# Residual loads, residual copies and output stores issued from GpSimd's DMA queue instead of the sync engine's, in a two-layer attention and FFN kernel

## The chip, the core and the metric

One Trainium2 chip, one of its cores. The metric is the device time of one execution in microseconds (us); less is better. The kernel before takes 1800.41 us (median of three runs, 1794.83 to 1801.01).

## What is computed

Sixteen independent sequences ("batches" b = 0 to 15) of 512 tokens and 128 features go through four residual steps:

```python
x = L0_attn_x                                   # (16, 512, 128) f32
x = x + _L0_attn_ref(_layernorm(x), ...)        # 16 heads of 8, softmax attention
x = x + _L0_ffn_ref(_layernorm(x), ...)         # silu(gate) * up, 384 hidden, then down
x = x + _L1_attn_ref(_layernorm(x), ...)        # 16 heads of 8, q and k RMS-normalised
x = x + _L1_ffn_ref(_layernorm(x), ...)         # base matmul + 8 gated LoRA experts of rank 8
```

Each `x +` is a residual: the value that went into the step has to be at hand when its result comes out.

## The kernel before, in words

The program is written engine by engine, by hand. Time is cut into slots of 64 units (`UNITS`); in each slot one attention `(layer, batch)` runs, in the order of `ATTENDS`: layer 0 of batches 0 and 1, then in turn layer 0 of batch b and layer 1 of batch b-2, and last layer 1 of batches 14 and 15. So in the middle two slots serve one batch. In each unit TensorE computes one 128x512 tile of scores (line 1237), ScalarE takes its exponential (L742), and TensorE multiplies it with the values (L1252); 26 units ahead of that, TensorE computes the same scores for the row maximum (L1227) and VectorE reduces them (L973). Between these units stand the "pieces" of the other steps: projections, layer norms, FFN, routing.

Every engine walks over the same unit counter t and, for each unit, issues what a table says is due: `PE_AT`, `ACT_AT`, `DVE_AT`, `POOL_AT`, `SP_AT`, one number (the unit in its group) for each piece. `due_table` turns a group's slot and the number into t. The numbers only set the order of instructions on each engine. What makes an engine wait is semaphores (`wait_ge`; `hold` on the queue that issues DMAs, which is the same wait).

Names that the change and the prediction speak of:

- `load_res0(b)`: loads x of batch b from HBM into `res[0]`, the residual of the first attention, as 128 partitions x 4 pieces of 512 bytes (256 KB). It waits until the addition that reads the same buffer for batch b-1 is done (`read["pr0"]`). Its reader is VectorE's `project_add(0)` (L1010, `x<-ps,res`).
- `copy_x2(b)`: copies x2 (the value after the first FFN) within SBUF into `res[1][b % 2]`, the residual of the second attention: 128 x 2 KB. It waits for `read["dn"]` (the addition that writes x2 of batch b) and for `read["pr1"]` of batch b-2. Its readers are `project_add(1)` of batch b and, as a guard against overwriting x2, `down_add(b + 1)`.
- `store(b)`: stores x3 of batch b to HBM, 128 x 4 pieces of 512 bytes. It waits for `read["out"]`, the final addition. `project_add(1)` of batch b+1, which overwrites x3, waits for `stored`, so for the landing of this store.
- On GpSimd (POOL): `norm_factors(k, b)` (L595 `rstd`, L597 `shift`), the factors of the four layer norms (nf0 to nf3), for which ScalarE's `apply_norm` (L748) waits; `up_mul` (L647, three for each batch); `normalise` (L616, `o_raw`), the division of an attention's result by the softmax sum; `residual1`, `residual2` (L602 to L610), `newton_round`, `scale_qk`, `mix` (L654).
- On SyncE (SP) in the kernel before: all other loads and stores of the loop, too. `max_rows` (L458) and `stack_half` (L452) feed the score matmuls, `rden_lines` (L472, L478) feeds `normalise`.

In the kernel before all three of the DMAs above stand in SP's walk:

```python
b = at(SP_DUE, "cpx2", t)
if b is not None:
    copy_x2(b)
```

and no DMA is issued by GpSimd anywhere.

Of the kernel before, what the change touches and what calls it, by code (L numbers as in the profile page):

```python
# [12 lines left out]
BATCH, SEQ, D = 16, 512, 128  # L13
# [62 lines left out]
SP_AT = {"A": {"rows0": -5, "rows1": 9, "rows2": 32, "rows3": 43, "den0": 40, "rden0": 52, "den1": 71,  # L76
# [3 lines left out]
         "S0": {"lx": 16},  # L80
         "M1": {"lr0": 52},
         "M2": {"out_p1": 21},
         "H1": {"cpx2": -16, "half0_p1": 38, "half1_p1": 42},
         "H1_tail": {"cpx2": 45, "half0_p1": 35, "half1_p1": 66},
         "E": {"store": 91}}

# [112 lines left out]
def build(nc, T, out_dram):  # L199
    ctx = ExitStack()  # L200
    with ctx:
# [167 lines left out]
        stored = sem("stored")  # L369
# [14 lines left out]
        def _(sp):  # L384
            def hold(sem, value):
                need(sp, sem, value)
# [32 lines left out]

            def load_res0(b):  # L420
                hold(read["pr0"], b)
                sp.dma_start(res_of(0, b)[:, :, :], tokens(b)).then_inc(res_copied[0], 16)

            load_res0(0)
            load_x(1)

# [54 lines left out]

            def copy_x2(b):

                hold(read["dn"], b + 1)
                hold(read["pr1"], b - 1)
                sp.dma_start(res_of(1, b)[:, :, :], x2[:, :, :]).then_inc(res_copied[1], 16)

            def store(b):

                hold(read["out"], b + 1)  # L490
                sp.dma_start(out_dram[b:b + 1].rearrange("a (t p) d -> p (a t) d", p=128), x3[:, :, :]
                             ).then_inc(stored, 16)

            parts_out(0, (0, 1), 0)
# [3 lines left out]
            for t in TIMES:  # L498
# [13 lines left out]
                if a is not None:  # L512
                    rden_lines(a[0], 1, a[1])
                b = at(SP_DUE, "lr0", t)
                if b is not None and b + 1 < BATCH:
                    load_res0(b + 1)
                b = at(SP_DUE, "out_p1", t)
# [20 lines left out]
                if a is not None:  # L538
                    max_rows(a[0], 3, a[1])
                b = at(SP_DUE, "cpx2", t)  # L540
                if b is not None:
                    copy_x2(b)
                b = at(SP_DUE, "half0_p0", t)
# [6 lines left out]
                if a is not None:  # L550
                    max_rows(a[0], 0, a[1])
                b = at(SP_DUE, "store", t)
                if b is not None:
                    store(b)
            hold(stored, 16 * BATCH)
# [3 lines left out]
        def _(pool):  # L559
# [47 lines left out]
            def residual2(l, n, b):  # L607
# [3 lines left out]
                                   ).then_inc(part2[2 * l + n], 1)  # L611

            def normalise(l, c, b):

                pool.wait_ge(rden_in[l], 16 * (2 * b + c + 1))
                pool.tensor_tensor(o_of(l, b)[:, c, :], o_of(l, b)[:, c, :], rden_all[:, c, :], ALU.mult  # L616
                                   ).then_inc(att_ready[l], 1)
# [46 lines left out]
            for n in (0, 1):  # L664
                residual1(0, n, 0)
                residual2(0, n, 0)
            norm_factors(0, 1)
            ones_in_k(1)
            clear_values(v_aug[1][0], 2)
            clear_values(v_aug[1][1], 3)  # L670
            for t in TIMES:
# [4 lines left out]
                for n in (0, 1):  # L676
                    b = at(POOL_DUE, f"sc{n}", t)
                    if b is not None:
                        scale_qk(n, b)
                a = at(POOL_DUE, "no1", t)  # L680
                if a is not None:
# [722 lines left out]
```

## Time and profile before

| | us |
|---|---|
| median of three runs (lowest, highest) | 1800.41 (1794.83, 1801.01) |
| the profiled execution: its own time | 1797.05 |
| its span, first to last instruction | 1795.3 |
| PE busy | 1684.5 (94% of the span) |
| DVE busy | 1543.6 (86%) |
| ACT busy | 1415.8 (79%) |
| POOL busy | 586.6 (33%) |
| DMA queue of SP and ACT (q1) | 27.6% of 16 engines |

How to read it: the span is what the trace shows; the execution's own time holds 1.75 us more around it. PE is TensorE, DVE VectorE, ACT ScalarE, POOL GpSimd, SP SyncE, which only issues DMAs; "SPq" is its queue. A busy share is an average over the start, the middle and the end of the kernel, which differ. The granted TensorE clock was 0.982 of full speed in the mean of this execution.

### The profile page before, as it was taken

What the parts mean: (1) busy time and instruction counts of PE and PEld (TensorE: products, weight loads), DVE (VectorE), ACT (ScalarE), POOL (GpSimd) and SP (SyncE); (2) the same over time, 40 slices, a digit from 0 to 9 for tenths busy, and PEclk for the clock granted to TensorE, in tenths of its full rate; (3) what the DMA queues carried; (4) which work ended last, traced back from release to release, by engine and by line L of the source; (5) the groups of instructions that cost most, each with busy time, mean ns of one, the idle gap of its engine ahead of it and who ended that gap; (6) DMA issues with size and microseconds to landing.
All of it is one profiled execution on the core that took longest, in us unless ns stands there. A gap on an engine that the chain in (4) does not pass through costs nothing.

```text
span 1795.3 us, 32451 instructions
## 1 busy us (share of the span) xinstructions
PE 1684.5 (94%) x10962; PEld 633.9 (35%) x10962; DVE 1543.6 (86%) x3347; ACT 1415.8 (79%) x2922; POOL 586.6 (33%) x840
## 2 busy tenths in 40 slices
PE   5999999999999999999999999999999999999995
PEld 2233333434333343333334333343433334334333
DVE  4988899898898989889898989989899898887981
ACT  2778788787978878787887988878797887777872
POOL 4224234151423324233242423415142332423311
PEclk8899999999999999999999999999999999999996
DMA  5232414223142322404232140422314142122310
GB/s 121 67 85 71 116 38 120 68 83 104 32 121 55 121 61 73 114 27 129 58 114 66 56 128 24 120 71 79 104 32 120 55 121 55 46 59 78 87 36 25
DMA packets 164024, 140.97 MB, mean 79 GB/s; under 512 B 40778, under 2 KB 145428, under 8 KB 163860
## 3 DMA queue, kind: packets, MB, share of 16 engines
q1 hardware_dynamic: 162084, 137.92, 27.6%
q8 instruction: 88, 1.44, 0.3%
q10 hardware_dynamic: 1776, 0.98, 0.2%
q14 instruction: 76, 0.62, 0.1%
HBM read 76.99 MB, written 55.57 MB: 74 GB/s over the span
## 4 chain that ended last, share of the span: by engine, by line
PE 62%; DVE 29%; issue 3%; ACT 2%; DMA 2%; SPq 1%; POOL 1%; DVEq 0%; ACTq 0%; POOLq 0%
DVE neg_max L973 20%; PE ps L1252 19%; PE ps L1237 14%; PE ps L1227 8%; PE ps L1273 7%; PE ps L1184 5%; PE ps L1266 3%; PE ps L1317 3%; DVE bn L949 2%; PE ps L1278 2%; DVE x L1010 2%; PE ps L1323 2%; DVE neg_high L979 1%; ACT probs L742 1%; DVE mv L957 1%
## 5 line engine op out<-in xcount | busy, mean ns | idle before, releaser
L973 DVE TENSOR_REDUCE neg_max<-ps 128x1 f32<-128x512 f32 x2048 | 1299.8, 682 | 100.2 <-PE ps L1227 91.1
L742 ACT ACTIVATE probs<-ps 128x512 f32<-128x512 f32 x2048 | 1093.3, 600 | 232.7 <-PE ps L1237 230.4
L1227 PE MATMUL ps<-k_stack,q_stack 48*128 48x512 bf16 x2048 | 679.1, 388 | 42.9 <-DVE neg_max L973 31.9
L1237 PE MATMUL ps<-q_stack,k_stack 50*128 50x512 bf16 x2048 | 632.1, 383 | 7.6 <-ACT probs L742 3.1
L1252 PE MATMUL ps<-probs,v_aug 128*32 128x512 f32 x4096 | 548.5, 608 | 0.7 <-ACT o_raw L718 0.7
L1237 PEld LDWEIGHTS ps<-q_stack,k_stack 50*128 50x128 bf16 x2048 | 148.1, 94 | 530.0 <-ACT probs L742 249.4
L1227 PEld LDWEIGHTS ps<-k_stack,q_stack 48*128 48x128 bf16 x2048 | 153.4, 93 | 227.4 <-DVE neg_max L973 202.1
L595 POOL TENSOR_TENSOR rstd<-vpe,half_neg 128x4 f32<-128x4 f32 x64 | 64.5, 1009 | 351.6 <-DVE vpe L964 351.5
L647 POOL TENSOR_TENSOR ht<-up,gs 128x512 f32<-128x512 f32 x48 | 61.1, 1273 | 223.2 <-ACT up L718 223.2
L1252 PEld LDWEIGHTS ps<-probs,v_aug 128*32 128x32 f32 x4096 | 80.7, 108 | 143.2 <-issue 73.7
L748 ACT ACTIVATE xn<-x,shift,rstd 128x128 f32<-128x128 f32 x192 | 80.7, 486 | 37.8 <-POOL shift L597 37.8
L616 POOL TENSOR_TENSOR o_raw<-o_raw,rden_all 128x512 f32<-128x512 f32 x64 | 81.3, 1270 | 49.9 <-DMA rden_all<-rden_rows 49.4
L602 POOL TENSOR_TENSOR qp<-qf,qp 128x512 bf16<-128x512 f32 x32 | 37.0, 1157 | 165.0 <-ACT qp L718 165.0
L654 POOL TENSOR_TENSOR coef<-gating,rm 128x64 f32<-128x64 bf16 x64 | 16.7, 292 | 225.3 <-DVE gating L1073 225.3
L1278 PE MATMUL ps<-wo,o_raw 128*128 128x128 f32 x512 | 67.3, 286 | 8.7 <-POOL o_raw L616 7.9
L626 POOL TENSOR_TENSOR nw_t<-nw_y 128x128 f32<-128x128 f32 x48 | 19.1, 399 | 156.2 <-DVE nw_y L1045 153.8
L1278 PEld LDWEIGHTS ps<-wo,o_raw 128*128 128x128 f32 x512 | 61.2, 196 | 18.3 <-issue 12.0
L1022 DVE SCALAR_TENSOR_TENSOR gs<-th,ps 128x512 f32<-128x512 f32 x48 | 32.7, 682 | 35.3 <-POOL ht L647 35.3
L1184 PE MATMUL ps<-ident,xn 128*128 128x128 f32 x256 | 44.1, 298 | 17.1 <-ACT xn L748 16.7
L718 ACT ACTIVATE up<-ps 128x512 f32<-128x512 f32 x48 | 28.7, 597 | 37.0 <-PE ps L1273 36.9
L1273 PE MATMUL ps<-xnt,w_up 128*128 128x256 f32 x192 | 54.3, 405 | 0.5 <-DVE gs L1022 0.5
L1010 DVE TENSOR_TENSOR x<-ps,x 128x512 f32<-128x512 f32 x32 | 22.0, 688 | 37.3 <-PE ps L1317 21.6
(117 smaller groups left out, 1579.5 us busy)
## 6 DMA issues: line engine op xcount, KB each, us to landing
rden_all<-rden_rows SPq DMA_DIRECT2D x64, 256.0 KB
q_rows<-qp SPq DMA_DIRECT2D x32, 384.0 KB, 2.9
k_rows<-kp SPq DMA_DIRECT2D x32, 384.0 KB, 2.9
q_stack<-q_rows SPq DMA_DIRECT2D x64, 192.0 KB, 3.8
k_stack<-k_rows SPq DMA_DIRECT2D x64, 192.0 KB, 4.8
q_stack<-q_rows SPq DMA_DIRECT2D x64, 144.0 KB, 2.9
k_stack<-k_rows SPq DMA_DIRECT2D x64, 144.0 KB, 3.3
q_rows<-qp SPq DMA_DIRECT2D x32, 256.0 KB, 3.1
```

Source lines behind the costliest of these rows:

```text
L595: pool.tensor_tensor(rstd[k][:, :], vpe[k][:, :], half_neg[:, :], ALU.pow).then_inc(rstd_ready[k], 1)
L616: pool.tensor_tensor(o_of(l, b)[:, c, :], o_of(l, b)[:, c, :], rden_all[:, c, :], ALU.mult).then_inc(att_ready[l], 1)
L647: pool.tensor_tensor(ht[:, c, :], up[:, :], gs[:, :], ALU.mult).then_inc(ht_done, 1)
L742: act.activation(probs[:, g % RING, :], home("score", (l, b, u)), ACT.Exp).then_inc(exps, 1)
L748: last = act.activation(xn[k][:, t, :], x[:, t, :], ACT.Identity, bias=shift[k][:, t:t + 1], scale=rstd[k][:, t:t + 1])
L973: dve.tensor_reduce(neg_max[l][:, pair // 2, col:col + 1], home("max", (l, b, n)), AX.X, ALU.max, negate=True).then_inc(max_taken, 1)
L1184: return pe.transpose(dst, src, ident[0:n, 0:n])
L1227: pe.matmul(home("max", (l, b, m)), q_stack[l][row:row + KROWS, pair, tok:tok + 128], k_stack[l][row:row + KROWS, pair, :], start=True, st ...
L1237: pe.matmul(home("score", (l, b, u)), k_stack[l][row:row + AROWS, pair, tok:tok + 128], q_stack[l][row:row + AROWS, pair, :], start=True, ...
L1252: last = pe.matmul(acc[32 * j:32 * j + 32, :], v_of(l, b)[:, kt, 8 * e + 2 * group + pp, :], probs[:, (g + j) % RING, :], start=(s == 0 an ...
L1273: return pe.matmul(dst[:, 256 * half:256 * half + 256], w, xt[:, 256 * half:256 * half + 256], start=True, stop=True)
L1278: last = pe.matmul(by_tile(dst)[:, t, :], o_of(l, b)[:, c, 128 * t:128 * t + 128], wo[l][:, c, :], start=c == 0, stop=c == 1)
```

## The change

The three functions move, with their waits, from SyncE's program to GpSimd's. In the tables `lr0`, `cpx2` and `store` keep their numbers and go from `SP_AT` to `POOL_AT`. The first `load_res0(0)`, which SyncE issued right after the weights, now stands on GpSimd behind the residual steps of batch 0 and ahead of the layer norm factors of batch 1. Within a unit, GpSimd issues them behind `scale_qk` and ahead of `normalise(.., 1, ..)`.

```diff
            "M1": {"nr0": 66, "nr1": 66, "nr2": 67, "nf1": 27, "um0": 27, "um1": 33, "um2": 38, "nf2": 55,
+                "lr0": 52},
...
-           "E": {"nf3": 32, "mix": 48}}
+           "E": {"nf3": 32, "mix": 48, "store": 91},
+           "H1": {"cpx2": -16},
+           "H1_tail": {"cpx2": 45}}
...
-         "M1": {"lr0": 52},
-         "H1": {"cpx2": -16, "half0_p1": 38, "half1_p1": 42},
-         "H1_tail": {"cpx2": 45, "half0_p1": 35, "half1_p1": 66},
-         "E": {"store": 91}}
+         "H1": {"half0_p1": 38, "half1_p1": 42},
+         "H1_tail": {"half0_p1": 35, "half1_p1": 66}}
...
+            def hold(sem, value):
+                need(pool, sem, value)
...
+            def load_res0(b):
+                hold(read["pr0"], b)
+                pool.dma_start(res_of(0, b)[:, :, :], tokens(b)).then_inc(res_copied[0], 16)
+
+            def copy_x2(b):
+
+                hold(read["dn"], b + 1)
+                hold(read["pr1"], b - 1)
+                pool.dma_start(res_of(1, b)[:, :, :], x2[:, :, :]).then_inc(res_copied[1], 16)
+
+            def store(b):
+
+                hold(read["out"], b + 1)
+                pool.dma_start(out_dram[b:b + 1].rearrange("a (t p) d -> p (a t) d", p=128), x3[:, :, :]
+                             ).then_inc(stored, 16)
...
                 residual2(0, n, 0)
+            load_res0(0)
             norm_factors(0, 1)
...
+                b = at(POOL_DUE, "cpx2", t)
+                if b is not None:
+                    copy_x2(b)
+                b = at(POOL_DUE, "store", t)
+                if b is not None:
+                    store(b)
+                b = at(POOL_DUE, "lr0", t)
+                if b is not None and b + 1 < BATCH:
+                    load_res0(b + 1)
```

The same functions and calls are taken out of SyncE's program. Three places on GpSimd, in the order in which its instructions stand (semaphores that each waits for in brackets; line numbers of the changed file differ, so L647 is L645 there, L595 is L570, L616 is L614).

**GpSimd, first FFN of batch 0, before.** `ht` is `up_mul`; the first `rstd` pair is nf0 of batch 3, the second nf2 of batch 0.

```order
L647 TENSOR_TENSOR ht<-up,gs 128x512 [waits u2_read,g2_read]
L595 TENSOR_TENSOR rstd<-vpe,half_neg 128x4 [waits var_ready0]
L597 TENSOR_TENSOR shift<-neg_mean,rstd 128x4 [waits rstd_ready0]
L595 TENSOR_TENSOR rstd<-vpe,half_neg 128x4 [waits var_ready2]
L597 TENSOR_TENSOR shift<-neg_mean,rstd 128x4 [waits rstd_ready2]
```

**The same place in the change:**

```order
L645 TENSOR_TENSOR ht<-up,gs 128x512 [waits u2_read,g2_read]
L603 DMA res<-x 128x512 [waits dn_read]
L570 TENSOR_TENSOR rstd<-vpe,half_neg 128x4 [waits var_ready0]
L572 TENSOR_TENSOR shift<-neg_mean,rstd 128x4 [waits rstd_ready0]
L597 DMA res<-in_L_attn_x 128x4x128 [waits pr0_read]
L570 TENSOR_TENSOR rstd<-vpe,half_neg 128x4 [waits var_ready2]
L572 TENSOR_TENSOR shift<-neg_mean,rstd 128x4 [waits rstd_ready2]
```

The copy of x2 of batch 0, with its wait for `dn`, now stands ahead of nf0 of batch 3, and the load ahead of nf2 of batch 0.

**GpSimd, first FFN of a batch in the middle, before:**

```order
L647 TENSOR_TENSOR ht<-up,gs 128x512 [waits u1_read,g1_read]
L647 TENSOR_TENSOR ht<-up,gs 128x512 [waits u2_read,g2_read]
L595 TENSOR_TENSOR rstd<-vpe,half_neg 128x4 [waits var_ready2]
L597 TENSOR_TENSOR shift<-neg_mean,rstd 128x4 [waits rstd_ready2]
L595 TENSOR_TENSOR rstd<-vpe,half_neg 128x4 [waits var_ready0]
L597 TENSOR_TENSOR shift<-neg_mean,rstd 128x4 [waits rstd_ready0]
```

**The same place in the change:**

```order
L645 TENSOR_TENSOR ht<-up,gs 128x512 [waits u1_read,g1_read]
L645 TENSOR_TENSOR ht<-up,gs 128x512 [waits u2_read,g2_read]
L608 DMA out_x<-x 128x4x128 [waits out_read]
L597 DMA res<-in_L_attn_x 128x4x128 [waits pr0_read]
L570 TENSOR_TENSOR rstd<-vpe,half_neg 128x4 [waits var_ready2]
L572 TENSOR_TENSOR shift<-neg_mean,rstd 128x4 [waits rstd_ready2]
L603 DMA res<-x 128x512 [waits pr1_read,dn_read]
L570 TENSOR_TENSOR rstd<-vpe,half_neg 128x4 [waits var_ready0]
L572 TENSOR_TENSOR shift<-neg_mean,rstd 128x4 [waits rstd_ready0]
```

A store and a load stand between the last `up_mul` and nf2, and the copy between nf2 and nf0.

**GpSimd, the last two batches, in the change** (before, the same rows stand there without the DMAs; `coef` is `mix`, the second `o_raw` of each pair releases the projection of the second attention):

```order
L614 TENSOR_TENSOR o_raw<-o_raw,rden_all 128x512 [waits rden_in1] x2
L608 DMA out_x<-x 128x4x128 [waits out_read]
L570 TENSOR_TENSOR rstd<-vpe,half_neg 128x4 [waits var_ready3]
L572 TENSOR_TENSOR shift<-neg_mean,rstd 128x4 [waits rstd_ready3]
L652 TENSOR_TENSOR coef<-gating,rm 128x64 [waits ct_read,gate_ready]
L652 TENSOR_TENSOR coef<-gating,rm 128x64 x3
L614 TENSOR_TENSOR o_raw<-o_raw,rden_all 128x512 [waits rden_in1] x2
L608 DMA out_x<-x 128x4x128 [waits out_read]
```

The stores of batches 13 and 14 stand behind the second `o_raw` of batch 14 and of batch 15; on SP they stood behind `rden_all<-rden_rows` of the same batch, which is ahead of that `o_raw`.

## Rows read from the trace of the kernel before

**Rows 1.** The page: busy times, and the chain that ended last by engine

```profile
PE 1684.5 (94%) x10962; PEld 633.9 (35%) x10962; DVE 1543.6 (86%) x3347; ACT 1415.8 (79%) x2922; POOL 586.6 (33%) x840
...
PE 62%; DVE 29%; issue 3%; ACT 2%; DMA 2%; SPq 1%; POOL 1%; DVEq 0%; ACTq 0%; POOLq 0%
```

**Rows 2.** Waits by pair, whole span: us in total, times, longest

```profile
PEld ps L1237 <- DMA q_stack<-m_parts: 6.0, 7, 1.0
...
PEld ps L1227 <- DMA k_stack<-k_rows: 3.9, 4, 1.7
```

**Rows 3.** Waits of SP's own DMA queue, whole span, same columns

```profile
SPq L458 <- ACT m_parts L718: 452.2, 121, 11.0
...
SPq L491 <- DVE x L1010: 26.7, 1, 26.7
SPq L486 <- DVE x L1010: 4.4, 1, 4.4
```

**Rows 4.** Issue ns min/median/max, first and last start: L422, L491; landing; longest issue

```profile
L422 SPq DMA_DIRECT2D res<-in_L_attn_x x16: 400/401/587, 15.3 to 1572.6; - x16
...
L491 SPq DMA_DIRECT2D out_x<-x x16: 387/499/1601, 325.3 to 1792.6; - x16
DMA to landing us min/median/max: 2.3/4.4/4.7
...
4.52 4.08 SPq L389 DMA_DIRECT2D qk_bias<-in_L_attn_bk  x1
```

**Rows 5.** Timeline (start us, us, what) of batch 0's first FFN: POOL, ACT, DVE, PE

```profile
135.44 1.00 POOL L595 TENSOR_TENSOR rstd<-vpe,half_neg 128x4 f32<-128x4 f32 x1
136.52 0.20 POOL L597 TENSOR_TENSOR shift<-neg_mean,rstd 128x4 f32<-128x4 f32 x1
...
136.84 0.87 ACT L748 ACTIVATE xn<-x_in,shift,rstd 128x128 f32<-128x128 f32 x2
137.61 1.07 ACT L742 ACTIVATE probs<-ps 128x512 f32<-128x512 f32 x2
...
139.68 0.69 DVE L1010 TENSOR_TENSOR x<-ps,x 128x512 f32<-128x512 f32 x1 [1.41 <-PE ps L1317]
...
140.89 0.39 PE L1237 MATMUL ps<-q_stack,k_stack 50*128 50x512 bf16 x1
```

**Rows 6.** Timeline of a batch in the middle: DVE, POOL, ACT, DVE

```profile
959.05 0.68 DVE L1010 TENSOR_TENSOR x<-ps,x 128x512 f32<-128x512 f32 x1
...
976.79 1.28 POOL L647 TENSOR_TENSOR ht<-up,gs 128x512 f32<-128x512 f32 x1 [2.93 <-ACT up L718]
985.15 1.01 POOL L595 TENSOR_TENSOR rstd<-vpe,half_neg 128x4 f32<-128x4 f32 x1 [7.08 <-DVE vpe L964]
...
990.62 1.01 POOL L595 TENSOR_TENSOR rstd<-vpe,half_neg 128x4 f32<-128x4 f32 x1 [4.19 <-DVE vpe L964]
...
986.47 1.65 ACT L748 ACTIVATE xn<-x,shift,rstd 128x128 f32<-128x128 f32 x4 [0.52 <-POOL shift L597]
...
1028.00 0.68 DVE L1010 TENSOR_TENSOR x<-ps,res 128x512 f32<-128x512 f32 x1
```

**Rows 7.** Timeline of batch 15's first-FFN layer norm: POOL, ACT

```profile
1626.14 1.01 POOL L595 TENSOR_TENSOR rstd<-vpe,half_neg 128x4 f32<-128x4 f32 x1 [0.46 <-DVE vpe L964]
...
1627.46 1.65 ACT L748 ACTIVATE xn<-x,shift,rstd 128x128 f32<-128x128 f32 x4 [1.09 <-POOL shift L597]
```

**Rows 8.** Timeline and chain of the last two batches' second projections: POOL, DVE

```profile
1729.37 1.26 POOL L616 TENSOR_TENSOR o_raw<-o_raw,rden_all 128x512 f32<-128x512 f32 x1 [13.18 <-DMA rden_all<-rden_rows]
...
1733.80 0.68 DVE L1010 TENSOR_TENSOR x<-ps,res 128x512 f32<-128x512 f32 x1
...
1768.82 1.26 POOL L616 TENSOR_TENSOR o_raw<-o_raw,rden_all 128x512 f32<-128x512 f32 x1 [12.96 <-DMA rden_all<-rden_rows]
...
1774.12 0.69 DVE L1010 TENSOR_TENSOR x<-ps,res 128x512 f32<-128x512 f32 x1 [10.77 <-PE ps L1278]
```

**Rows 9.** Timeline of the start: POOL's layer norm factors of batch 1

```profile
26.19 1.01 POOL L595 TENSOR_TENSOR rstd<-vpe,half_neg 128x4 f32<-128x4 f32 x1 [3.95 <-DVE vpe L964]
```

More of the change, by code:

```diff
@@ L418, in load_x @@
                 sp.dma_start(x_in[:, :, :], tokens(b)).then_inc(x_loaded, 16)
[L420 to L424, printed above, removed]
             load_x(1)
@@ L480, in rden_lines @@
                              ).then_inc(rden_in[l], 16)
[L482 to L492, printed above, removed]
             parts_out(0, (0, 1), 0)
@@ L513, in _ @@
                     rden_lines(a[0], 1, a[1])
-                b = at(SP_DUE, "lr0", t)
-                if b is not None and b + 1 < BATCH:
-                    load_res0(b + 1)
                 b = at(SP_DUE, "out_p1", t)
@@ L539, in _ @@
                     max_rows(a[0], 3, a[1])
-                b = at(SP_DUE, "cpx2", t)
-                if b is not None:
-                    copy_x2(b)
                 b = at(SP_DUE, "half0_p0", t)
@@ L551, in _ @@
                     max_rows(a[0], 0, a[1])
-                b = at(SP_DUE, "store", t)
-                if b is not None:
-                    store(b)
             hold(stored, 16 * BATCH)
@@ L611, in residual2, with tokens @@
                                    ).then_inc(part2[2 * l + n], 1)
+            def hold(sem, value):
+                need(pool, sem, value)
+            def tokens(b):
+                x = T["L0_attn_x"]
+                return x[b:b + 1].rearrange("a (t p) d -> p (a t) d", p=128)
+            def load_res0(b):
[9 more added lines that the diff above has]
+                             ).then_inc(stored, 16)
             def normalise(l, c, b):
```

2 rows, old and new, of the table POOL_AT are left out of this document.

## The prediction

> **What bounds the kernel now.** I read the page first. TensorE is busy 94% of the span and VectorE 86%, and the chain that ended last runs through them for 62% and 29% of it, through DMAs for 2% and SP's queue for 1% [rows 1]. GpSimd is busy a third of the time. So a change of queues can win only where somebody waits for a DMA, and can lose only where GpSimd, made later, holds up the chain.
>
> Next the waits. TensorE waits for DMAs that SP issues 6.0 us over 7 times for the maximum rows and 3.9 us over 4 times for the k stack [rows 2], in 1795 us. SP's own queue is an engine that waits: 452.2 us for the maximum rows alone. The three functions that leave it held it up twice in the whole run, 4.4 us for the first copy and 26.7 us for the last store, behind which nothing stands [rows 3]. SP is no bottleneck, and the moved DMAs block nothing on it.
>
> Then, at each place where the change puts a DMA on GpSimd, I read the timeline for three things: when GpSimd gets there, when the semaphore that the DMA waits for comes, and how long GpSimd stands idle before the next instruction.
>
> **What leaves SP.** 48 issues, of 0.40 us for a load and 0.50 us for a store in the median [rows 4], some 23 us of SP's time. I cost this at nothing: SP's 452.2 us of waiting for the maximum rows hide it [rows 3], and what stood behind a moved DMA on SP waited for something else.
>
> **The price of one DMA on GpSimd.** No row shows one, so I bound it. Below: what SP takes for the same DMA, 0.40 us. Above: the longest issue in the trace, 4.08 us on SP for a list of 4-byte pieces [rows 4]. GpSimd does this with its cores as it does arithmetic, and its ordinary instruction over 128 x 512 elements takes 1.28 us [rows 6]. I take 1.2 us for the copy (128 pieces) and 2.0 us for a load or a store (512 pieces), nearer to that row than to the upper end, and call the latter g. From the end of an issue to landing I take 2.3 us, the fastest landing of this store on SP [rows 4]. So a store issued by GpSimd to an idle set of engines lands 4.3 us after GpSimd reaches it. The Trainium skill, page "DMA: Bandwidth & Descriptors", section "Latency and other measured facts", gives about 0.6 us to the first byte for SP's path and about 1 us for GpSimd's. By that alone a store would land only 0.4 us later than on SP, and the sum below would be about 4 us, the stall of batch 0 and 0.4 us at the end; no run here shows it yet.
>
> **The middle, 12 batches: nothing.** Behind the third `up_mul` GpSimd stands idle for 7.08 us until VectorE has the variance for nf2 [rows 6]. Into this gap come the store and the load. Both their semaphores came long before (the final addition is over at 959.73, the gap begins at 978.07; the first projection's addition stands ahead of the FFN). They take 2 x 2.0 = 4.0 us of 7.08. The copy comes into the next gap, 4.19 us: its semaphore, `dn`, is the addition from which the variance itself is made, so it is there; 1.2 of 4.19 us. What this covers must stay covered: ScalarE waits 0.52 us for nf2's `shift` already [rows 6], so everything over 7.08 us is paid in full. The next addition that waits for the copy and for a store, at 1028.00, comes 36 us after the second gap begins [rows 6].
>
> **Batch 0: a new wait.** Here the order is another: the copy, waiting for `dn`, stands ahead of nf0 of batch 3. Before, GpSimd did nf0 at 135.44 and ScalarE used it at 136.84. `dn` is there when the addition at 139.68 ends, at 140.37 [rows 5]. The change: 140.37 + 1.2 (copy) + 1.28 (nf0, 135.44 to 136.72) = 142.85, so ScalarE stands still 6.0 us. Behind the standing instruction are the exponentials. `dn` itself does not need them, so this is a wait and no deadlock. The score tile that TensorE computed at 140.89 needs a bank that the first exponential behind the standing instruction frees; that is ready at 142.9 + 0.8 + 0.6 = 144.3 [rows 5]: **+3.4 us**. The load behind nf0 ends at about 144.9 and nf2 at 146.1, when the late ScalarE (144.0 + 3.4) is not there yet: nothing more. Bounds: 2 us if the queues behind catch up, 6 us if all is passed on.
>
> **Batch 15's first layer norm.** The store of batch 12 stands ahead of nf1, with 0.46 us of gap [rows 7]: nf1 comes 2.0 - 0.46 = 1.5 us late. ScalarE waits for it already (1.09 us). TensorE runs on with the tiles in its banks meanwhile; I take half a microsecond off for that: **+1.0 us** (0 to 3.6).
>
> **The last two projections.** `project_add(1)` waits for the store of the batch before. Batch 14: GpSimd ends `o_raw` at 1730.63, the store lands at 1734.9, and the addition stood at 1733.80: **+1.1 us** (0 to 3.2). Batch 15: 1770.09 + 4.3 = 1774.4 against 1774.12: **+0.3 us** (0 to 2.4) [rows 8].
>
> **The last store.** SP issued it at 1792.60 [rows 4] and the span ended at 1795.3, 2.7 us later; now 4.3 us: **+1.6 us** (0 to 3.7).
>
> **The start.** The first load on GpSimd falls into a gap before nf0 of batch 1, which is 3.95 us long [rows 9]: nothing.
>
> **The sum.** 3.4 + 1.0 + 1.1 + 0.3 + 1.6 = **+7.4 us**. On the profiled execution, 1797.05 + 7.4 = 1804.5. Its time lies 3.4 us under the median of the three runs, so on the median it is 1800.41 + 7.4 = 1807.8. I say **1808 us**. A difference of 0.5%, 9.0 us, is about what a measurement of this kernel can tell from no change.
>
> **Rivals.**
>
> *A, GpSimd becomes late in every batch.* It decides at 3.54 us for a DMA of 512 pieces, half of 7.08. At the upper bound, 4.08, nf2 is 1.08 us late in each of 12 batches, 13 us, and the other terms go to their upper ends: 3.4 + 3.6 + 3.2 + 2.4 + 3.7 = 16.3. Together +29 us: 1830. For it: four times as many pieces as the copy has, generated by a program. Against: every row of SP for the same shape is near 0.4 us. Chance 0.2.
>
> *B, the stalls of batch 0 and the tail are paid in full but the middle holds:* g near 3 us. Then 6 + 2.5 + 2.1 + 1.3 + 2.6 = +14.5: 1815. Chance 0.17.
>
> *C, faster than before.* Small transfers on SP's queue no longer stand behind 256 KB ones. The place is TensorE's waits for the maximum rows and the k stack, 9.9 us in all [rows 2]. It decides if these waits go and a GpSimd DMA costs as little as on SP (0.4 us), so that batch 0 alone costs: 3.4 - 9.9 = -6.5: 1794, and if the stall of batch 0 is caught up too, 1790. Against: the waits are few, 11 in 1795 us, while the moved DMAs stood on SP 48 times. Chance 0.07 (over 0.5%: 0.04).
>
> *D, nothing to see:* the stall of batch 0 is caught up, and the rest is tenths: +1 to +4 us: 1803 at 2.5. Chance 0.16.
>
> My forecast (+4 to +11 us) has 0.4. The range leaves out most of A and part of C: 1797 to 1822. The likeliest case alone is 1804 to 1811. Within 0.5% are the rest of C (0.03), D (0.16), 0.28 of the forecast and 0.03 of B: 0.50. Slower by more: A (0.20), 0.14 of B and 0.12 of the forecast: 0.46. Faster: 0.04.
>
> **What would show it.** Right: DMAs on GpSimd of 1 to 3 us; a ScalarE wait of some 6 us at L748 near 137 us for a GpSimd `shift`; the wait of nf2 for VectorE shorter than 7.08 us, and not gone; VectorE waiting for the store at the last two `x<-ps,res`; no other change from one batch to the next in the middle. Wrong: nf2 without a wait for VectorE, or ScalarE waiting much over 0.52 us for it in every batch (rival A); no stall at 137 us; or TensorE's waits for q_stack and k_stack gone (rival C).

## The result and the profile after

The changed kernel takes 1804.8 us in the median of 20 runs (1801.9 to 1810.9), the kernel before 1798.8 us in 20 (1794.6 to 1803.2). The ratio is **1.0031, with a 95% interval of 1.0022 to 1.0040**: 5.6 us slower (4.0 to 7.2), within the 0.5% that the prediction called no change. The prediction had +7.4 us and 1808 us, with a range of 1797 to 1822. The profiled execution takes 1805.4 us with a span of 1803.7, 8.4 us more than the profiled span before (1795.3).

The page of the changed kernel:

```profile
span 1803.7 us, 32451 instructions
...
PE 1686.2 (93%) x10962; PEld 633.8 (35%) x10962; DVE 1544.2 (86%) x3347; ACT 1417.9 (79%) x2922; POOL 622.9 (35%) x888
...
q1 hardware_dynamic: 142884, 125.34, 25.8%
q0 software_dynamic: 3840, 12.59, 2.2%
...
PE 61%; DVE 29%; issue 3%; DMA 3%; ACT 2%; POOL 1%; SPq 1%; DVEq 0%; POOLq 0%; ACTq 0%
```

The chain is made of the same engines as before. GpSimd's busy time has gone up by 36 us, about what its 48 DMAs take; each line of the change has its durations in the view by source line (L597 load, L603 copy, L608 store):

```profile
L597 POOL DMA_DIRECT2D res<-in_L_attn_x x16: 753/758/934, 22.2 to 1583.5; - x16
...
DMA to landing us min/median/max: 3.4/3.6/4.7
...
L603 POOL DMA_DIRECT2D res<-x x16: 594/598/631, 142.2 to 1700.1; - x16
...
DMA to landing us min/median/max: 2.3/2.3/4.1
...
L608 POOL DMA_DIRECT2D out_x<-x x16: 814/828/829, 343.5 to 1800.2; - x16
...
  DVE x L1018: 0.9, 1
...
DMA to landing us min/median/max: 2.8/2.8/4.1
```

So a DMA on GpSimd costs 0.60 us for 128 pieces and 0.76 to 0.83 us for 512, where SP takes 0.54 for the copy and 0.40 and 0.50 for load and store [rows 4], and I had put in 1.2 and 2.0. Each kind takes nearly the same time wherever it stands, and the longest of the 48 took 0.93 us (the first load, 22.2 us), so nothing held GpSimd up while it issued. The landing, which this view counts from the start of the issue, moved both ways in the median: from 2.9 to 3.6 us for a load, from 4.4 to 2.8 for a store [rows 4], and it stayed at 2.3 for the copy. Why the stores land sooner from GpSimd's queue was not tested. Now the three places of the prediction. Batch 0, the timeline of the changed kernel:

```profile
142.19 0.63 POOL L603 DMA_DIRECT2D res<-x  x1 [5.19 <-DVE x L1018]
142.84 1.06 POOL L570 TENSOR_TENSOR rstd<-vpe,half_neg 128x4 f32<-128x4 f32 x1
...
144.22 0.88 ACT L756 ACTIVATE xn<-x_in,shift,rstd 128x128 f32<-128x128 f32 x2 [5.76 <-POOL shift L572]
...
145.72 0.45 PE L1245 MATMUL ps<-q_stack,k_stack 50*128 50x512 bf16 x1 [3.25 <-ACT probs L750]
...
147.53 1.92 PE L1260 MATMUL ps<-probs,v_aug 128*32 128x512 f32 x8
```

The copy waits 5.19 us for `dn` with nf0 of batch 3 behind it, ScalarE stands 5.76 us, and TensorE 3.25 us for the exponential's bank. The last row was not foreseen: eight matmuls that take 1.06 us elsewhere take 1.92. The windows of TensorE (length in us, busy time and instructions, granted clock, DMA share, GB/s) say why; a clock of 1.00 is 2.4 GHz, 0.50 is 1.2:

```profile
142.00:145.00 3.00, 0.47 (x8) 1.00 0.56 164
145.00:148.00 3.00, 2.28 (x12) 0.65 0.37 98
148.00:151.00 3.00, 2.29 (x15) 0.78 0.00 0
```

After standing still, TensorE runs at 1.2 GHz for part of the next six microseconds (in the kernel before the clock is 1.00 in all three windows). The copy itself begins 0.31 us after the addition that it waited for has ended (141.19 + 0.69 = 141.88 us). The middle, again the timeline (compare [rows 6]):

```profile
983.61 0.83 POOL L608 DMA_DIRECT2D out_x<-x  x1
984.44 0.76 POOL L597 DMA_DIRECT2D res<-in_L_attn_x  x1
990.76 1.03 POOL L570 TENSOR_TENSOR rstd<-vpe,half_neg 128x4 f32<-128x4 f32 x1 [5.56 <-DVE vpe L972]
...
992.11 1.66 ACT L756 ACTIVATE xn<-x,shift,rstd 128x128 f32<-128x128 f32 x4 [0.55 <-POOL shift L572]
```

The gap of 7.08 us has shrunk to 5.56 and still ends with VectorE; ScalarE's wait is 0.55 for 0.52 us. It is so in all twelve batches in which a store and a load stand there: VectorE ends GpSimd's wait each time, after 5.55 to 5.57 us, and ScalarE waits 0.55 to 0.56 us. The tail, of which [rows 7, 8] are the counterparts:

```profile
1631.69 0.82 POOL L608 DMA_DIRECT2D out_x<-x  x1
...
1633.90 1.66 ACT L756 ACTIVATE xn<-x,shift,rstd 128x128 f32<-128x128 f32 x4 [1.47 <-POOL shift L572]
...
1737.20 0.82 POOL L608 DMA_DIRECT2D out_x<-x  x1
...
1741.40 0.69 DVE L1018 TENSOR_TENSOR x<-ps,res 128x512 f32<-128x512 f32 x1 [0.89 <-DMA out_x<-x]
...
1781.43 0.69 DVE L1018 TENSOR_TENSOR x<-ps,res 128x512 f32<-128x512 f32 x1 [10.46 <-PE ps L1286]
...
1799.25 0.69 DVE L1018 TENSOR_TENSOR x<-ps,x 128x512 f32<-128x512 f32 x1 [6.87 <-PE ps L1276]
1800.24 0.81 POOL L608 DMA_DIRECT2D out_x<-x  x1 [6.73 <-DVE x L1018]
```

ScalarE waits 1.47 for 1.09 us, the addition of batch 14 waits 0.89 us for the store, that of batch 15 waits for TensorE, and the span ends 4.45 us behind the start of the last addition, for 3.42 before. Of that 1.0 us, 0.27 lie ahead of the issue (the store begins 0.30 us behind the end of the addition, SP's began 0.03 us behind it) and 0.47 in the landing (2.78 for 2.31 us).

**Where the time went.** The kernel has 64 additions into x on VectorE, at the same places of both programs. The start of one here, less the start of the same one in the profile of before, is the lag that has built up by then. I read it for every kernel below but e7 and e8, which have sections of their own; the heads of the columns are the times of five such additions in the kernel before, and the last column is the difference of the spans:

| kernel | 139.7 us | 209.2 | 282.1 | 1491.9 | 1791.9 | span |
|---|---|---|---|---|---|---|
| changed | 1.5 | 5.1 | 5.0 | 6.5 | 7.4 | 8.4 |
| e1, copy of batch 0 behind | 1.2 | 1.2 | 1.0 | 0.9 | 3.3 | 4.3 |
| e2, wait alone | 0.5 | 3.4 | 4.5 | 5.5 | 4.6 | 4.6 |
| e3, first load on SP | -1.5 | 2.2 | 1.5 | 2.4 | 4.4 | 5.4 |
| e4, last stores on SP | -0.8 | 2.7 | 3.6 | 2.6 | 0.2 | 0.3 |
| e5, three mended | -0.6 | -0.7 | -1.4 | -1.2 | -3.2 | -3.1 |
| e6, gap plus two | 0.3 | 4.2 | 4.9 | 5.3 | 5.4 | 6.4 |
| e9, loads alone | 1.5 | 1.9 | 1.3 | 1.6 | 1.8 | 1.8 |
| e10, copies alone | -0.6 | 3.4 | 2.5 | 1.6 | 3.4 | 3.4 |
| e11, stores alone | 1.3 | 1.3 | 1.0 | 0.5 | 3.1 | 4.4 |
| e12, three mended again | 0.2 | 0.7 | 1.4 | 1.2 | 2.3 | 2.4 |

One row is one execution, and carries its scatter; the columns together tell more than any row.

### The profile page after: what moved, and what is told of

Its sections match the earlier page's. It is cut to its first block, busy times and chain, and to the rows that moved or that the text cites. A ratio compares the mean times of both kernels' runs of the same rounds, so it can differ in the third digit from the quotient of the medians.

```text
span 1803.7 us, 32451 instructions
## 1 busy us (share of the span) xinstructions
PE 1686.2 (93%) x10962; PEld 633.8 (35%) x10962; DVE 1544.2 (86%) x3347; ACT 1417.9 (79%) x2922; POOL 622.9 (35%) x888
## 3 DMA queue, kind: packets, MB, share of 16 engines
q1 hardware_dynamic: 142884, 125.34, 25.8%
q0 software_dynamic: 3840, 12.59, 2.2%
## 4 chain that ended last, share of the span: by engine, by line
PE 61%; DVE 29%; issue 3%; DMA 3%; ACT 2%; POOL 1%; SPq 1%; DVEq 0%; POOLq 0%; ACTq 0%
DVE neg_max L981 20%; PE ps L1260 19%; PE ps L1245 13%; PE ps L1235 8%; PE ps L1281 7%; PE ps L1192 5%; PE ps L1274 3%; PE ps L1325 3%; DVE bn L957 2%; DVE x L1018 2%; PE ps L1286 2%; PE ps L1331 2%; DVE neg_high L987 1%; ACT probs L750 1%; DMA rden_all<-rden_rows 1%
## 5 line engine op out<-in xcount | busy, mean ns | idle before, releaser
L570 POOL TENSOR_TENSOR rstd<-vpe,half_neg 128x4 f32<-128x4 f32 x64 | 65.6, 1025 | 311.1 <-DVE vpe L972 310.9
L645 POOL TENSOR_TENSOR ht<-up,gs 128x512 f32<-128x512 f32 x48 | 61.2, 1275 | 223.8 <-ACT up L726 223.8
L614 POOL TENSOR_TENSOR o_raw<-o_raw,rden_all 128x512 f32<-128x512 f32 x64 | 81.4, 1272 | 46.5 <-DMA rden_all<-rden_rows 46.2
L1192 PE MATMUL ps<-ident,neg_max 128*32 128x128 f32 x128 | 36.3, 284 | 19.6 <-DVE x L1018 10.3
```

The source lines that it names most:

```text
L570: pool.tensor_tensor(rstd[k][:, :], vpe[k][:, :], half_neg[:, :], ALU.pow).then_inc(rstd_ready[k], 1)
L645: pool.tensor_tensor(ht[:, c, :], up[:, :], gs[:, :], ALU.mult).then_inc(ht_done, 1)
L1192: return pe.transpose(dst, src, ident[0:n, 0:n])
```

## Experiments

Theory 1: the change costs a sum of stalls, each at its place (batch 0, the tail), and nothing else. Its rivals: a price of GpSimd's DMAs in every batch; a gain on SP's queue that the stalls hide. Each ratio is taken against the kernel before in the same session, whose median was 1798.0 us for e1 to e4, 1797.5 for e5 to e8 and 1797.9 for e9 to e12, so differences between kernels are read from ratios and not from the medians.

### The stall of batch 0

e1 moves the one copy. Against the changed kernel:

```diff
                 b = at(POOL_DUE, "cpx2", t)
-                if b is not None:
+                if b is not None and b > 0:
                     copy_x2(b)
...
                     norm_factors(2, b)
+                    if b == 0:
+                        copy_x2(b)
```

> The changed kernel, with the first copy of the second residual alone moved on GpSimd from ahead of nf0 of batch 3 to behind nf2 of batch 0. Theory 1 (the time is a sum of stalls, each at its own place, and the largest is this wait): ScalarE no longer stands 5.76 us at xn<-x_in near 138 us; the first additions of batches 0 and 1 near 141 and 209 us, which came 1.5 and 5.1 us late against the kernel before, both come 1.5 us late or less, and the 3.6 us between them do not come back elsewhere: about 1801.3 us where the changed kernel has 1804.8. Rival (GpSimd's DMAs cost something in every batch, and the wait of batch 0 is caught up by slack that the next batches have anyway): the addition near 209 comes earlier, but by 600 us the lag is 5 us again, and the time stays within 1 us of 1804.8.

Measured: 1799.2 us, ratio 1.0014 (1.0006 to 1.0023), for the 1.0031 of the changed kernel: 3.1 us are back, as expected (the two intervals just touch). The lag is flat through batches 0 and 1 (1.2 us at 139.7 and at 209 us) and under 1.3 us up to 1576 us. Timeline of GpSimd, e1:

```profile
135.44 1.27 POOL L645 TENSOR_TENSOR ht<-up,gs 128x512 f32<-128x512 f32 x1 [2.93 <-ACT up L728]
136.68 1.00 POOL L570 TENSOR_TENSOR rstd<-vpe,half_neg 128x4 f32<-128x4 f32 x1
```

nf0 of batch 3 is back behind the `up_mul`, as in [rows 5]. ScalarE takes its factors at 138.08 us without a wait. Theory 1 holds; the rival that slack would catch the stall up is out.

e2 has the wait and no DMA. Against the kernel before:

```diff
                 b = at(POOL_DUE, "nf0", t)
                 if b is not None:
+                    if b == 3:
+                        need(pool, read["dn"], 1)
                     norm_factors(0, b)
```

> The kernel before, all DMAs on SP, with one wait added on GpSimd: for dn of batch 0, ahead of nf0 of batch 3. No DMA is moved. Theory 1 (the stall of batch 0 is the wait in GpSimd's order, the DMA itself only adds its 0.6 us): nf0 of batch 3 starts near 140.4 us, ScalarE stands 4.8 to 5.1 us before xn<-x_in, and the additions from 209 us on come 2.8 to 3.2 us late: about 1801.8 us against 1798.8. Rival (the stall is made by the DMA on GpSimd, by its descriptors or by the copy's reads of x2): ScalarE's wait is as long, but TensorE does not wait for it, and the addition at 209 us is less than 1 us late: 1799.

Measured: 1801.6 us, ratio 1.0023 (1.0012 to 1.0034). Timeline of GpSimd and TensorE, e2:

```profile
140.96 1.01 POOL L595 TENSOR_TENSOR rstd<-vpe,half_neg 128x4 f32<-128x4 f32 x1 [4.97 <-DVE x L1012]
...
143.79 0.37 PE L1239 MATMUL ps<-q_stack,k_stack 50*128 50x512 bf16 x1 [2.31 <-ACT probs L744]
...
145.51 1.93 PE L1254 MATMUL ps<-probs,v_aug 128*32 128x512 f32 x8
```

ScalarE stands 4.82 us, and TensorE 2.31 us where the changed kernel has 3.25: the DMA adds 0.9 us to the stall (0.63 for itself, the rest because it begins 0.31 us behind the addition's end, where nf0 alone begins 0.08 us behind it), the wait is the rest. The slow clock is there behind the stall too (1.93 us). From the addition at 139.7 us to that at 209.2 the lag grows by 2.9 us in e2, by 3.6 to 4.0 in the five kernels of the table with wait and copy (changed, e3, e4, e6, e10), and by -0.2 to 0.5 in the five without. So the wait alone makes some three quarters of the loss, and the copy behind it the rest.

By 282 us e2 has 4.0 us, but the 1.4 us that it gains between 209 and 236 us belong to no stall of batch 0. e4, e6 and e12 gain the same there, and e12 has no stall ahead of it; the changed kernel, e3 and e10 have the stall and gain nothing. Window of TensorE, e12:

```profile
215.00:220.00 5.00, 4.98 (x27) 0.70 0.11 31
```

The clock of the same window is 0.66 to 0.82 in e2, e4 and e6, and 1.00 in the kernel before. This is scatter of the clock, and it blurs the column at 282.1 us, where the six kernels with the wait have grown by 3.0 to 4.6 us, 3.8 in the mean, and the five without by -0.9 to 1.2, in the mean -0.1.

### The start

e3 has the first load back on SP, on a semaphore of its own. Against the changed kernel:

```diff
+            sp.dma_start(res_of(0, 0)[:, :, :], tokens(0)).then_inc(res_first, 16)
             load_x(1)
...
-            load_res0(0)
             norm_factors(0, 1)
```

> The changed kernel, with only the very first load of the first residual back on SP, where it stood. It asks where the 1.6 us come from by which the changed kernel is late at 112 us already. Theory 1 (the load on GpSimd costs nothing there, TensorE's clock fell earlier in that one execution: the matmuls at 28.9 us took 0.98 us for 0.56): this execution may have either start, and the lag at 112 us does not follow the load; the time is 1804 to 1805.5. Rival (the load on GpSimd near 22 us disturbs the start): the addition near 112.6 us is back within 0.3 us, the matmuls at 28.9 take 0.56 us, and the time is 1803.2.

Measured: 1802.6 us, ratio 1.0023 (1.0012 to 1.0034). That lies nearer to the rival's 1803.2 us than to the 1804 to 1805.5 of theory 1, and the rival's other two signs came as well in this one execution (fast matmuls at 28.3 us, the lag at 112.6 us gone); but the interval overlaps that of the changed kernel, so the time does not decide, and the other traces do. The 1.5 us by which the changed kernel is late at 112 us come from two pairs of matmuls at 28.9 us that turn the last weights. The timeline of the changed kernel:

```profile
28.93 1.62 PE L1206 MATMUL ps<-probs 128*128 128x384 f32 x2 [0.67 <-ACT probs L726]
```

That of e2, in which SP issues every DMA:

```profile
28.81 1.62 PE L1200 MATMUL ps<-probs 128*128 128x384 f32 x2 [0.67 <-ACT probs L720]
```

That of e4, in which GpSimd loads the residual as in the changed kernel:

```profile
22.20 0.95 POOL L608 DMA_DIRECT2D res<-in_L_attn_x  x1
...
28.89 0.88 PE L1218 MATMUL ps<-probs 128*128 128x384 f32 x2 [0.67 <-ACT probs L737]
```

The slow form is there without the load, and the fast one with it. Of the five executions in the table with the load on GpSimd's queue there, three have the slow form (changed, e1, e9), of the six without it two (e2, e11). The lag at 112.6 us is 0.5 to 1.6 us in those five and -1.4 to -0.4 in the other six: it follows the form of the matmuls and not the load. The record's granted clock does not resolve this place (it stands at 1.00 in the changed kernel while the matmuls take 1.8 times as long), so that it is the clock is read from durations alone. Small losses from the first load are bounded by e9 below, which has this load and the other 15 on GpSimd: its interval ends at 1.0004, 0.7 us.

### The tail

e4 leaves stores 0 to 11 on GpSimd and issues the last four from SP, on a semaphore of their own (the first hunk is in SP's loop, the second in GpSimd's):

```diff
+                b = at(POOL_DUE, "store", t)
+                if b is not None and b >= TAIL:
+                    store(b)
...
-                if b is not None:
+                if b is not None and b < TAIL:
                     store(b)
```

> The changed kernel, with the stores of batches 12 to 15 back on SP. Theory 1 (the tail pays for late stores): nf1 of batch 15 no longer stands behind a store (1.2 us of lag between 1611 and 1651 us go), the addition of batch 14's second projection no longer waits 0.89 us for the store (0.7 us), and the last store ends 1.0 us sooner: in all 2 to 3 us, 1802.3 us. Rival (these waits lie beside others, and only the last store's end counts): 1.0 us or less, 1803.8 to 1804.8.

Measured: 1800.9 us, ratio 1.0021 (1.0011 to 1.0031), 1.8 us under the changed kernel, a little less than expected and with overlapping intervals, so the timing alone does not show it. The rows do. Timeline of ScalarE, e4:

```profile
1629.61 1.65 ACT L767 ACTIVATE xn<-x,shift,rstd 128x128 f32<-128x128 f32 x4 [1.09 <-POOL shift L583]
```

Its wait is 1.09 us again [rows 7], and the span ends 3.5 us behind the start of the last addition (1792.12), as before. The lag from 1492 us to the end of the span, table, falls by 2.3 us; it rises by 1.9 in the changed kernel. Over all kernels of the table it rises by 1.1 to 3.9 us where the last stores are GpSimd's (changed, e1, e3, e6, e11; mean 2.7) and by -2.3 to 1.8 where they are SP's (the other six; mean -0.3): some 3 us, for 4.0 predicted. Part of it is the clock. In the changed kernel, e1 and e11, 1.2 us of the rise stand between the additions at 1611 and 1651 us, where ScalarE waits for nf1, and the granted clock between 1630 and 1640 us is 0.66 to 0.70. In e3 and e6, also with GpSimd's stores, it is 0.83 and the lag does not rise there; with the last stores on SP it is 0.83 to 1.00, and the lag changes by -1.5 to 0.0. How much of the 1.2 us the store makes is open.

### Is the middle free, and is anything gained?

e5 and e12 are one kernel, with the edits of e1, e3 and e4 together. 43 of the 48 DMAs are still on GpSimd (15 loads, 16 copies, 12 stores; the expectation says 42).

> The changed kernel with three DMAs or groups of them put where they hold up nothing: the first copy behind nf2 of batch 0, the first load and the stores of batches 12 to 15 back on SP. 42 of the 48 DMAs stay on GpSimd. Theory 1 (the change costs its stalls and nothing else, and relieves nothing): the time is that of the kernel before, 1798 within 1.5 us, a ratio of 0.9995 to 1.001. Rival C (SP's queue, relieved, gives TensorE's waits for the maximum rows and the k stack back, up to 9.9 us, and the stalls had hidden that): 1789 to 1794. Rival (GpSimd's DMAs cost something in every batch): 1800 or more, with a lag that grows steadily from 240 to 1600 us.

> The mended kernel a second time, since its first timing (1.0014, interval 1.0005 to 1.0024) and its first profile (a span of 1792.2 us, under that of before) speak for different things. Theory 1 (no cost is left but chance): a ratio of 1.000 to 1.001. Rival (each DMA on GpSimd keeps a small price in the middle): 1.0014 or more again, and a lag that grows from batch to batch in this profile too, which it did not in the first (-1.44 us at 282 us, -1.14 us at 1569 us).

Measured: 1799.5 us, ratio 1.0014 (1.0005 to 1.0024), and 1798.3 us, 0.9998 (0.9988 to 1.0008). The two intervals only just overlap, which shows how far a timing of this kernel can be trusted to a tenth of a per cent; their mean is 1.0006. The first is above theory 1's range, the second within it, and a cost of about 1 us that the three edits leave is not excluded. Neither is faster than the kernel before, so rival C is out. The gain that it hoped for is not there in the changed kernel either; waits by pair:

```profile
PEld ps L1245 <- DMA q_stack<-m_parts: 6.2, 7, 1.1
...
PEld ps L1235 <- DMA k_stack<-k_rows: 3.1, 4, 1.2
```

Before they were 6.0 and 3.9 us [rows 2], so 0.6 of the 9.9 us are gone, in one profile of each kernel. A price in every batch would show as a lag that grows between 282 and 1492 us. Over the eleven rows of the table it changes by -1.0 to 1.4 us, 0.1 in the mean, and e2, with no DMA on GpSimd, has one of the largest (1.0). So the 1.4 us that the changed kernel's profile gathered there are scatter as far as these rows can tell.

The parts alone, each made from the kernel before by moving one function and its call:

> The kernel before, with the 16 loads of the first residual alone on GpSimd; copies and stores stay on SP. Theory 1 (only waits at named places cost): a load is late for nobody, lag of the additions flat within 1 us (but for the 1.5 us of either sign that the start shows in any kernel), ratio 1.000 within 0.001. Rival (what is left in the mended kernel, a ratio of 1.0014, is a cost of GpSimd's DMAs that every batch pays): a ratio of 1.0005 to 1.001, the lag growing by 0.1 us in a batch.

> The kernel before, with the 16 copies of the second residual alone on GpSimd. Theory 1: the stall of batch 0, ScalarE standing some 5.5 to 5.8 us near 138 us, and a lag of 3.0 to 4.5 us from 282 us on that stays, 1.0017 to 1.0025: most of the whole change's 1.0031. Rival (the parts need one another: only with the load behind nf0 too does ScalarE's lateness pass to TensorE): a lag under 2 us.

> The kernel before, with the 16 stores alone on GpSimd. Theory 1: nothing at batch 0 and in the middle; ScalarE's wait for nf1 of batch 15 0.3 to 0.5 us longer, the addition of batch 14's second projection later by the wait for the store (0.7 to 1.0 us), the span ended 1.0 us later behind the last addition: 2 to 2.5 us, a ratio of 1.0010 to 1.0014. Rival (only the last store's end counts): 1.0005.

Measured: 0.9994 (0.9984 to 1.0004), 1.0011 (1.0002 to 1.0020) and 1.0007 (0.9996 to 1.0019). The loads cost nothing that the timing can see. The copies have the stall of batch 0, a lag that grows by 3.1 us there, of which the timing shows 2 us, less than I expected; e2, with the wait and no copy, timed 4 us, the mend e1 gave 3 us back, and these intervals overlap, so the profiles size this stall better than any one timing. The stores' timing does not tell 1.0010 from 1.0005; their profile has the tail's 3.9 us. The three add up to 1.0012, under the 1.0031 of the whole; each has 0.001 of uncertainty, so this is at the edge of chance, and whether the parts amplify each other is left open.

### How wide the gap is, and what lies beyond it

e6 and e7 fill the gap before nf2 in batches 1 to 12, e6 as shown and e7 with 4 in the place of each 2:

```diff
                     load_res0(b + 1)
+                    for n in range(2 if 1 <= b <= 12 else 0):
+                        need(pool, spare_set, 2 * (b - 1) + n)
+                        pool.memset(spare[:, :], 0.0).then_inc(spare_set, 1)
```

> The changed kernel, with two memsets of a spare 128x2048 tile (about 1.8 us each, 3.7 us together) on GpSimd behind the load in batches 1 to 12, in the gap before nf2. Theory 1 (the middle is free because of the gap, which is 5.56 us long after store and load): they fit, GpSimd still waits 1.8 us for VectorE before nf2, ScalarE's wait for shift stays 0.55 us, and the time is that of the changed kernel, 1804.8 within 1.5 us. Rival (GpSimd's time is paid in part at once, through the memory port that it shares with VectorE or through a late ScalarE): 12 x 1 to 3.7 us, 1817 to 1849.

> The same with four memsets, 7.4 us. Theory 1, and the sentence of the prediction that everything beyond the gap is paid in full: nf2 comes 7.4 - 5.5 = 1.9 us late in each of 12 batches, 12 x 1.9 = 23 us: 1828. Rival (ScalarE and the banks of TensorE absorb the first microseconds of lateness): 0 to 0.5 us for each batch, 1805 to 1811.

Measured: e6 1803.1 us, ratio 1.0031 (1.0021 to 1.0042), the changed kernel's own. Timeline of e6:

```profile
984.48 3.69 POOL L692 MEMSET spare<- 128x2048 f32 x2
990.04 1.04 POOL L572 TENSOR_TENSOR rstd<-vpe,half_neg 128x4 f32<-128x4 f32 x1 [1.88 <-DVE vpe L977]
...
991.39 1.65 ACT L761 ACTIVATE xn<-x,shift,rstd 128x128 f32<-128x128 f32 x4 [0.56 <-POOL shift L574]
```

44 us of work for GpSimd cost nothing that the timing can see. e7 takes 1839.4 us, 1.0233 (1.0215 to 1.0252): 36.3 us over the changed kernel by the ratios, 3.0 for each of twelve batches and not the 1.9 expected. Its timeline, in two batches:

```profile
1013.30 1.65 ACT L761 ACTIVATE xn<-x,shift,rstd 128x128 f32<-128x128 f32 x4 [2.38 <-POOL shift L574]
...
1015.09 0.63 PE L1197 MATMUL ps<-ident,xn 128*128 128x128 f32 x4 [1.89 <-ACT xn L761]
...
1015.97 1.06 PE L1265 MATMUL ps<-probs,v_aug 128*32 128x512 f32 x8
...
1123.35 0.70 PE L1197 MATMUL ps<-ident,xn 128*128 128x128 f32 x4 [1.88 <-ACT xn L761]
...
1124.53 1.93 PE L1265 MATMUL ps<-probs,v_aug 128*32 128x512 f32 x8
```

and its windows of TensorE:

```profile
1014.00:1020.00 6.00, 4.91 (x35) 1.00 0.15 51
...
1122.00:1128.00 6.00, 4.65 (x21) 0.72 0.13 46
```

ScalarE's wait grew by 1.8 us, as the sum has it, and TensorE stands 1.9 us in both batches. In the first the clock holds, and the lag of e7 grows by 1.9 us across this place (the additions at 982 and 1028 us). In the second it falls, the same eight matmuls take 1.93 for 1.06 us, and the lag grows by 3.1. Eleven batches have this stall of TensorE, 1.87 to 1.89 us each (batch 1 has no store in its gap, and a smaller excess): in two the matmuls behind it take 1.06 us and the lag grows by 1.8 and 1.9 us, in nine they take 1.66 to 1.94 us and the lag grows by 2.8 to 4.3, 3.2 in the mean. The rival, that banks absorb the first microseconds, is out; a stall costs more than its length, not less.

### The price of one DMA, alone

> The changed kernel, with twice five DMAs of the input into a spare tile behind the last store, one after the other, each waited for, first on GpSimd, then the same on SP: 128 pieces of 2 KB, 512 pieces of 512 bytes, 2048 pieces of 128 bytes, 128 pieces of 4 bytes, 16 pieces of 2 KB. It prices one DMA on each engine with nothing else going on. Theory (a fixed part of about 0.55 us and 0.4 to 0.6 ns for each piece, from the 0.60 us of the copy with 128 pieces and the 0.76 us of the load with 512): 0.60, 0.76, 1.4, 0.60 and 0.55 us on GpSimd. Rival (GpSimd's time goes with the bytes, not the pieces): 0.76, 0.76, 0.76 and less for the two small ones. Landing 2.0 to 2.8 us behind the end of the issue on GpSimd; on SP 0.4 to 0.5 us for the first two and longer for 2048 pieces, 2.0 to 2.5 us to landing. The whole adds 20 x 3 = 60 us to the time, which says nothing here.

Timelines of GpSimd and of SP's queue, e8; what precedes is the DMA before, waited for:

```profile
1800.50 0.56 POOL L760 DMA_DIRECT2D spare<-in_L_attn_x  x1 [2.26 <-DMA out_x<-x]
1803.70 0.76 POOL L763 DMA_DIRECT2D spare<-in_L_attn_x  x1 [2.63 <-DMA spare<-in_L_attn_x]
1807.17 1.16 POOL L766 DMA_DIRECT2D spare<-in_L_attn_x  x1 [2.71 <-DMA spare<-in_L_attn_x]
...
1833.61 0.34 SPq L544 DMA_DIRECT2D spare<-in_L_attn_x  x1
1836.24 0.39 SPq L547 DMA_DIRECT2D spare<-in_L_attn_x  x1
1839.06 0.62 SPq L550 DMA_DIRECT2D spare<-in_L_attn_x  x1
```

On GpSimd 128, 512 and 2048 pieces take 0.56, 0.76 and 1.16 us, the 128 pieces of 4 bytes 0.56, the 16 of 2 KB 0.53; on SP 0.34, 0.39, 0.62, 0.33 and 0.34. The time goes with the pieces and not with the bytes, with a fixed half microsecond, and less than in proportion (0.5 ns for a piece up to 512, 0.26 ns beyond). From one start to the next, landing included, GpSimd takes 3.20 us where SP takes 2.63 (128 pieces), and 3.47 where SP takes 2.82: 0.6 us more. Half of that is the way to the landing, 2.9 us for SP's 2.5 to 2.6 with 128 pieces and 3.2 to 3.4 for 2.8 to 2.9 with 512 (view by source line, from the start of the issue); the other 0.3 us stand between the landing and the start of GpSimd's next DMA, where SP has 0.02, the same 0.3 us as behind the additions in the changed kernel. The first packet of data starts 1.27 us behind the start of GpSimd's issue and 0.97 behind SP's (128 pieces), 1.47 and 1.05 (512). The Trainium skill, page "DMA: Bandwidth & Descriptors", section "Latency and other measured facts", has 0.4 us between the two paths (1 us and 0.6 us to the first byte); the trace agrees on the difference, 0.3 and 0.4 us to the first packet, though each of its two times is some 0.3 to 0.5 us longer. The fit of its section "Anatomy of one DMA — SWDGE (gpsimd) path", 2.0 us plus the bytes over 436 KB/us, gives an estimate of 2.6 us for 256 KB, for which this kernel has 2.9 from issue to landing in 2 KB pieces and 3.2 to 3.4 in 512-byte pieces. This is one execution, with two passes over each shape that agree within 0.2 us.

## Why the prediction was right

Point by point, with its own steps:

- **What leaves SP: nothing.** Right. TensorE's waits for SP's DMAs are nearly what they were (9.3 us for 9.9), and the mended kernel is not faster.
- **The price.** Mis-sized, by a factor of two or more: 2.0 us for a load or store measured 0.76 to 0.83, 1.2 for the copy 0.60. The true value lay between the bounds, near the lower one, and the sign "DMAs on GpSimd of 1 to 3 us" did not come. The 2.3 us for the landing was misread too: the view counts it from the start of the issue, not from its end. From start to landing a store took 2.8 us in the median, and 4.1 at most, for the 4.3 assumed. What the sum lacked is that GpSimd begins a DMA 0.3 us behind the event that it waits for.
- **The middle: nothing.** Right, and with more room: the gap is 5.56 us, e6 puts 3.7 us more into it for nothing. (From the second gap to the addition at 1028.00 it is 41.6 us and not 36, which changes nothing.) That what exceeds the gap is paid in full fell short: 1.9 us cost 3.0 in the mean (e7), because TensorE's clock falls behind the stall. Rival A, priced at 13 us for 1.08 us in 12 batches, may thus have been too cheap; no run tried that size.
- **Batch 0: +3.4 us.** Right in place, cause and size. ScalarE stood 5.76 us (6.0 predicted), TensorE's scores came 3.3 us late against the addition ahead of them (3.4), and mended it gives back 3.1 us by the ratios. That the size came out is luck in part: the copy was put in 0.6 us too dear, and the 0.3 us ahead of its start and the slow clock behind the stall were left out, and these errors oppose each other.
- **Batch 15's nf1: +1.0.** ScalarE's wait grew by 0.4 us, the lag around it by 1.2 in three profiles of five and not in the other two. **Batch 14: +1.1.** 0.89 us of waiting, 0.7 of lag; its store took 4.1 us to land, nearly the 4.3 put in, because a price too high and a landing too short cancelled. **Batch 15: +0.3.** Nothing; its store landed in 2.8 us and TensorE came last, so one of the two waits for a store that I had named as a sign did not come. **The last store: +1.6.** 1.0. In all 2.1 us by their rows for 4.0 predicted; the eleven profiles have about 3 between their two groups.
- **The start: nothing.** Right as far as can be told: the profile is 1.5 us late by then, but that follows the matmuls at 28.9 us and not the load, and the loads alone cost at most 0.7 us (e9).
- **The sum.** 3.6 (batch 0, up to the addition at 209.2 us) + 0.4 + 0.7 + 1.0 = 5.7 us, and the ratio gives 5.6. So close a fit is chance: the interval is 4.0 to 7.2 us, and the three parts alone add up to 2.2. The 2.7 us by which this profile's span is later are nearly all the start and the middle (1.5 and 1.4), its own scatter. Of the 3.0 us between 1807.8 and the measured 1804.8, 1.6 come from the kernel before, whose first three runs lay that much above its later median.
- **The rivals.** A needed 3.54 us for a DMA and the measured one is 0.83. B needed 3 us for one. C needed waits that did not go. D, the stall of batch 0 caught up, is refuted by e1.

## What to carry to other kernels

A DMA moved to GpSimd's queue costs its issue only where GpSimd has no gap for it, so the question is not what the issue takes but what stands behind it in program order: here a copy that waits for a late semaphore, ahead of an unrelated layer norm, made about half of the loss by its wait alone (2.9 of 5.6 us), and its own issue added 0.9 us to TensorE's stall. Look first for the batch in which the order differs from the others (the first, the last), and move the waiting instruction behind the one that others need. When a stall of TensorE is priced, add that the clock may fall behind it: the 1.9 us of e7 cost 3.2 in most batches. And compare profiles at several places, since the clock alone moved single profiles by 1.4 us between two additions (e12 at 209 to 236 us).

## What the runs showed that I had not expected

- A stall of 1.9 us of TensorE is followed by matmuls at 1.2 GHz in nine of eleven batches (eight matmuls up to 1.94 for 1.06 us), and costs 3.2 us; the same stall with the clock held cost 1.8 to 1.9. The Trainium skill, page "TensorE: Matmul & The Clock Gate", section "Part 1: The HAM clock gate (the "warmup" mystery)", names the same two levels and says that how many matmuls run slowly at a kernel's start differs between runs of one kernel. The traces agree: windows at 1.00 and at 0.50 (e2, 145 to 148 us) are 2.4 and 1.2 GHz, and e5 and e12, one kernel, have 1.00 and 0.70 between 215 and 220 us.
- The clock is also part of the kernel's scatter: the same matmuls at 28.9 us took 0.88 or 1.62 us in kernels that do not differ there, and that alone moves a whole profile by 1.5 us.
- A DMA on GpSimd that has to wait begins 0.3 us behind the event (0.31 behind the addition of batch 0, 0.30 behind the last addition, 0.28 behind a landing in e8); on SP it is 0.02 to 0.03 us.
- The 48 moved DMAs are 19,200 packets fewer on SP's queue (162,084 to 142,884) and only 3,840 on GpSimd's, 80 for each instead of 400 in the mean, for the same 12.59 MB. It had no effect on the time that these runs could see.
